# The sliding-window band cut out by two selections a job on GpSimd, in place of mask products on TensorE

## The chip, the cores and the metric

The kernel runs on one core of a Trainium2 chip (the program is built for one device). A core has five engines that run on their own instruction queues and meet only at semaphores: PE (TensorE, products), DVE (VectorE), ACT (ScalarE), POOL (GpSimd) and SP (SyncE, which here only issues DMAs). The metric is the device time of one execution in microseconds (us), as the median of several runs.

## The reference, cut to what matters

A block of attention for 8 sequences of 512 tokens with 128 features, and behind it a routed feed-forward layer over all 4096 tokens. In the attention 16 heads of 8 dimensions go two ways: a causal linear attention with a second-order feature map, and a softmax over a sliding window of 64 earlier tokens:

```python
def sliding_window_attention(q, k, v):
    B, T, H, D = q.shape
    scale = 1.0 / math.sqrt(D)
    t = jnp.arange(T)
    allowed = (t[None, :] <= t[:, None]) & (t[None, :] >= t[:, None] - WINDOW)
    scores = jnp.einsum('bqhd,bkhd->bhqk', q, k) * scale
    scores = jnp.where(allowed[None, None], scores, -jnp.inf)
    attn = jax.nn.softmax(scores, axis=-1)
    out = jnp.einsum('bhqk,bkhd->bqhd', attn, v)
    return out.reshape(B, T, H * D)
...
lin = linear_attention_causal(q_phi, k_phi, v).reshape(B, T, D_MODEL)
win = sliding_window_attention(q, k, v)
out = jnp.concatenate([lin, win], axis=-1) @ Wout
```

The feed-forward layer sends each token to two of eight experts (four with a GELU, four with a basis of squared tanh), and adds the weighted results.

## The kernel before

**Two stages.** The first half of the program (until about 530 us of the profile) is the attention, batch by batch, with the routing decisions of the batch before woven in. The second half gathers tokens by expert, tile by tile, and runs the experts. Only the first half is touched.

**The order of a batch** is written out by hand as a list of words, `ORDER`, which every engine's program follows. A capital letter is the next step of a series of this batch, a word with `-` belongs to the tail of the batch before, one with `+` to the front of the batch after:

```python
ORDER = """
M L M L M -ytr L M L M L -ycT M L M M -out L L L M -coef2 L M L +stats M +aggr P +coef L L M L L M L
M M L -h2norm P L +hT -h2T M L -logit L +q L +k mT Y L L -store P L -choose W W W +u +v -rank P
-total W +stacks +residual W -gapexp W W P W Y W W -weights +xload P W W W W Y W W P -scatter P
""".split()
```

`M` are 16 steps of scores for the running maximum ("max": four groups of four heads, four chunks of 128 keys), `L` 24 steps of the linear attention ("lin"), `W` 16 steps of the window ("win"), `P` the eight products with the values ("pv"), `Y` and `ytr` transposes of their results. pv 0 to pv 3 take the four head groups of the linear part, pv 4 to pv 7 those of the window. So from the first `W` to the last `P` a batch runs: three win jobs, u, v and rank, pv 3, the fourth win job of group 0, three of group 1, pv 4, the fourth of group 1, a transpose, two of group 2, pv 5, two of group 2, two of group 3, a transpose, two of group 3, pv 6, scatter, pv 7.

**A ring of PSUM.** Each step that PE computes for another engine is a job: it takes the next of three slots (two banks each) of `ring`. PE fills it and raises `filled`, the reader empties it and raises `freed`, and PE waits for `freed` before it fills the slot again.

**A win job** has 128 keys on the partitions, four heads, and up to 192 queries (`WQ`; 128 in the last chunk, j = 3). For each of the two banks PE first writes a mask of -1e30 outside the band with a product of the identity and `mask_win` (L1394) and then adds the scores of two heads (L1398). ACT takes the exponential into `Pb` (L846), a buffer with two halves, by n % 2; outside the band it comes out as zero. ACT's first job of a group waits for the pv that read that half last. pv (L1431) multiplies `Pb` with the values and a column of ones; for the window it waits until ACT has freed the group's last win job, and for the engine that copies `pv` out (`y_sb`: L1046 on DVE for even n, L853 on ACT for odd n).

**POOL** in the attention: for each head group of the linear part it zeroes the upper triangle of the diagonal blocks (L673, released by ACT's `freed`; raises `pd_ready`, for which pv 0 to pv 3 wait), the coefficients and the normalised rows of the next batch (`+coef`: L600 to L610, L619), the same for the feed-forward part of the batch before (`-coef2`: L600 to L610, L689), the residual of the next batch (`+residual`: L626, waits for a store of SP) and the scatter of routing records (`-scatter`: eight indirect DMAs, L698, waits for `rec_ready` of DVE). `link` makes the next POOL instruction wait for the one before through the semaphore `pool_chain`. DVE reads the max jobs with its own mask, `mask_max` (L1034), and does the routing (L1098 to L1137).

## Time and profile before

| | |
|---|---|
| time, median of 3 runs | 1073.29 us (1070.0 to 1078.98) |
| time of the profiled execution | 1078.86 us |
| its span | 1077.1 us |
| mean granted clock of PE | 0.907 of 2.4 GHz |
| busy in the span | PE 852.7, DVE 519.9, ACT 551.2, POOL 509.4 us |

The profile shows one execution. A row of a timeline gives the start and the duration in us, the engine, the line of the program, the operation, what is written and what is read (buffer numbers left out), how many instructions are merged in the row, and in brackets for how long the engine sat idle before and what ended that. PE's matmuls are pipelined: a row's duration holds the way through the array, and how fast they follow one another is seen from the starts.

### The profile page before, as it was taken

How to read it: one execution, taken by the hardware profiler on the slowest of the kernel's cores; microseconds unless marked ns; L12 is line 12 of the kernel's file. 1: busy time of each engine (PE TensorE's matmuls, PEld its weight loads, DVE VectorE, ACT ScalarE, POOL GpSimd, SP SyncE). 2: the span in 40 equal slices, each digit the busy share in tenths (PEclk: the TensorE clock that was granted, in tenths of full speed). 3: DMA queues.
4: the chain of work that ended last, by engine and by line, in shares of the span. 5: the costliest groups of instructions: out<-in, count | busy, mean ns of one | idle time of the engine just before them, and what ended most of it. 6: DMA issues, size and time to landing. Idle time of an engine off the chain costs nothing.

```text
span 1077.1 us, 23744 instructions
## 1 busy us (share of the span) xinstructions
PE 852.7 (79%) x8106; PEld 659.0 (61%) x8107; DVE 519.9 (48%) x2114; ACT 551.2 (51%) x744; POOL 509.4 (47%) x648
## 2 busy tenths in 40 slices
PE   3399997979999898989605776767999899996980
PEld 1267675756767676666503554455889877985870
DVE  5554647355564637464330111125766745766340
ACT  1476665656666665656302423326655746765240
POOL 7140635245364635242437778745545544653022
PEclk9699999989999999999856978978999988997985
DMA  2403040301213040301004545562213433332013
GB/s 44 106 2 86 5 112 2 112 5 46 71 29 89 2 116 2 111 6 32 21 11 102 87 75 82 83 179 58 70 45 98 103 92 98 101 100 52 2 13 94
DMA packets 91071, 68.50 MB, mean 64 GB/s; under 512 B 42892, under 2 KB 83274, under 8 KB 89034
## 3 DMA queue, kind: packets, MB, share of 16 engines
q1 hardware_dynamic: 74010, 55.10, 18.4%
q0 software_dynamic: 16912, 11.35, 7.5%
q8 instruction: 101, 1.65, 0.7%
q14 instruction: 48, 0.39, 0.1%
HBM read 46.86 MB, written 21.37 MB: 63 GB/s over the span
## 4 chain that ended last, share of the span: by engine, by line
PE 46%; POOL 19%; issue 13%; DVE 7%; DMA 7%; ACT 5%; another core or an unknown queue 1%; POOLq 1%; SPq 0%; DVEq 0%; ACTq 0%
PE pv L1618 8%; PE pv L1431 8%; POOL acc_d L730 7%; PE ring L1591 5%; PE ring L1394 4%; DMA acc_d<-stack,srec 4%; PE ring L1398 4%; DVE masked L1034 3%; PE ring L1442 2%; POOL stack L720 2%; ACT Pb L830 2%; PE ring L1353 2%; PE pv L1554 2%; PE ring L1322 2%; POOL c L609 2%
## 5 line engine op out<-in xcount | busy, mean ns | idle before, releaser
L730 POOL DMA_INDIRECT acc_d<-stack,srec x84 | 135.0, 1607 | 117.2 <-DVE stack L1221 79.5
L1034 DVE CUSTOM_DVE_ANT_0 masked<-ring,mask_max 128x192 bf16<-128x192 f32 (+1 forms) x512 | 141.6, 337 | 73.4 <-PE ring L1353 61.7
L1232 DVE SCALAR_TENSOR_TENSOR stack<-stack 128x512 f32<-128x512 f32 x240 | 156.9, 690 | 36.7 <-ACT stack L907 25.4
L907 ACT ACTIVATE stack<-ring,kprm 128x512 f32<-128x512 f32 x160 | 111.1, 795 | 100.0 <-DVE stack L1232 99.2
L1618 PE MATMUL pv<-stack 128*128 128x128 f32 x1120 | 136.5, 285 | 12.2 <-DVE stack L1232 7.3
L1618 PEld LDWEIGHTS pv<-stack 128*128 128x128 f32 x1120 | 133.6, 201 | 15.9 <-DVE stack L1232 8.3
L1591 PE MATMUL ring<-stack 128*128 128x256 f32 x560 | 136.9, 409 | 2.4 <-DVE stack L1232 2.4
L673 POOL TENSOR_SCALAR_AFFINE_SELECT Pb<-Pb 128x1024 f32<-128x1024 f32 x64 | 69.0, 1094 | 135.3 <-ACT Pb L830 135.2
L836 ACT ACTIVATE Pb<-ring 128x768 f32<-128x768 f32 x128 | 101.2, 812 | 61.0 <-PE ring L1382 56.6
L1591 PEld LDWEIGHTS ring<-stack 128*128 128x128 f32 x560 | 115.1, 207 | 26.7 <-DVE stack L1232 5.9
L698 POOL DMA_INDIRECT slot_d<-rec,pos x64 | 62.4, 974 | 119.6 <-DVE pos L1130 102.6
L1431 PE MATMUL pv<-Pb,vaug 128*16 128x128 f32 (+3 forms) x2816 | 118.4, 317 | 0.0
L846 ACT ACTIVATE Pb<-ring 128x768 f32<-128x768 f32 (+1 forms) x128 | 89.8, 757 | 23.4 <-PE ring L1398 20.9
L1431 PEld LDWEIGHTS pv<-Pb,vaug 128*16 128x16 f32 x2816 | 74.3, 97 | 35.7 <-issue 19.3
L1353 PE MATMUL ring<-stack 128*128 128x192 f16 (+1 forms) x512 | 63.2, 250 | 30.4 <-DMA stack<-ones 18.4
L830 ACT ACTIVATE Pb<-ring 128x1024 f32<-128x1024 f32 x64 | 63.5, 1023 | 45.0 <-PE ring L1373 37.9
L1394 PE MATMUL ring<-mask_win,identb 128*128 128x384 bf16 x256 | 81.1, 327 | 0.1
L1398 PE MATMUL ring<-stack 128*128 128x192 f16 (+1 forms) x512 | 80.5, 239 | 0.0
L1382 PE MATMUL ring<-stack 128*128 128x384 f16 (+2 forms) x384 | 64.7, 282 | 14.5 <-ACT Pb L830 7.6
L720 POOL DMA_INDIRECT stack<-n_d,grec x40 | 67.2, 1681 | 16.1 <-issue 16.1
L878 ACT ACT_TABLE_LOAD x11 | 14.1, 1283 | 106.1 <-PE pv L1554 60.9
L1353 PEld LDWEIGHTS ring<-stack 128*128 128x128 f16 x512 | 38.9, 102 | 45.4 <-issue 21.1
(205 smaller groups left out, 1261.0 us busy)
## 6 DMA issues: line engine op xcount, KB each, us to landing
stack<-L_ffn_kan_sl_W SPq DMA_DIRECT2D x20, 1024.0 KB, 5.2
stack<-hl_d SPq DMA_DIRECT2D x24, 256.0 KB
Pb<-L_ffn_mlp_W SPq DMA_DIRECT2D x22, 256.0 KB, 2.8
stack<-hl_d SPq DMA_DIRECT2D x24, 128.0 KB
hl_d<-hi SPq DMA_DIRECT2D x7, 384.0 KB, 3.1
hl_d<-lo SPq DMA_DIRECT2D x7, 384.0 KB, 3.7
xb<-L_attn_x SPq DMA_DIRECT2D x9, 256.0 KB, 5.0
acc_d<-res SPq DMA_DIRECT2D x8, 256.0 KB, 2.5
```

What stands on the lines that cost most here:

```text
L730: pool.indirect_dma_start(acc_d, bass.IndirectOffsetOnAxis(ap=srec[:, kind, u, q, 0:1], axis=0), src[:, u % 2, q, :], None, compute_op=ALU ...
L836: act.activation(Pb[:, n % 2, 2048 + 768 * hd:2048 + 768 * (hd + 1)].rearrange("p (k q) -> p k q", k=2), slot(job)[:, :, 0:384], ACT.Squar ...
L846: act.activation(Pb[:, n % 2, 768 * c:768 * (c + 1)].rearrange("p (k j q) -> p k j q", k=2, j=2)[:, :, :, 0:wq], slot(job)[:, :, 0:384].re ...
L907: act.activation(sig[z][:, g % SIGS, :], src, ACT.Sigmoid, bias=bias, scale=scale).then_inc(k_sig[z], 1)
L1034: red = dve.tensor_tensor_reduce(masked[:, (NT * n + c) % SLOTS, hh, k0:WQ], slot(job)[:, hh // 2, WQ * (hh % 2) + k0:WQ * (hh % 2 + 1)], ...
L1232: dve.scalar_tensor_tensor(basis[z][:, g % G, :], s_, -1.0, s_, ALU.add, ALU.mult).then_inc(k_bas[z], 1)
L1353: mm = pe.matmul(slot(job)[:, bk, WQ * jj + k0:WQ * (jj + 1)], sq[:, h, P * c:P * (c + 1)], sk[:, h, P * c - WIN + k0:P * (c + 1)], start= ...
L1394: pe.matmul(slot(job)[:, bk, 0:2 * WQ], identb[:], mask_win[:].rearrange("p a q -> p (a q)"), start=True, stop=True)
L1398: mm = pe.matmul(slot(job)[:, bk, WQ * jj:WQ * jj + wq], sk[:, h, P * c:P * (c + 1)], sq[:, h, P * c:P * c + wq], start=False, stop=True, ...
L1431: mm = pe.matmul(pv[32 * j:32 * j + 16, n % 2, q0:q0 + w], vaug[:, p, c, HG * (n % NHG) + j, :], src[:, j, :], start=(c == 0 and x_ == 0), ...
L1591: mm = pe.matmul(ring[:, 0, q // 2, F2 * (q % 2):F2 * (q % 2 + 1)], basis[0][:, g, P * q:P * (q + 1)], kw[u % 2][:, F2 * g:F2 * (g + 1)], ...
L1618: mm = pe.matmul(pv[:, 1, P * q:P * (q + 1)], basis[1][:, g % G, P * q:P * (q + 1)], kw[u % 2][:, 2048 + D * g:2048 + D * (g + 1)], start= ...
```

## The change

The window's mask goes from ahead of the exponential to behind it. PE no longer writes a mask into the banks; its score products start each bank region afresh. ACT's exponentials are the same. POOL, as soon as ACT has freed a win job, sets two parts of it in `Pb` to zero: queries ahead of the key (columns 0 to 127 of each head) and queries more than 64 behind it (columns 64 to 191, or 64 to 127 in the last chunk). The second selection waits for the first, since they overlap. POOL raises `pw_ready` with each job, and pv 4 to pv 7 wait for it in place of ACT's `freed`. `mask_win` and the three instructions that make it are gone.

```diff
@@ -122,7 +122,6 @@
         identf = sb("identf", [P, P])
         identb = sb("identb", [P, P], BF16)
         mask_max = sb("mask_max", [P, WQ], BF16)
-        mask_win = sb("mask_win", [P, 2, WQ], BF16)
         block = sb("block", [P, P])
         consts = sb("consts", [P, 5, NT])
         w_raw = sb("w_raw", [P, 3, D])
@@ -267,6 +266,7 @@
         mT_ready = sem("mT_ready")
         mrow_loaded = sem("mrow_loaded")
         pd_ready = sem("pd_ready")
+        pw_ready = sem("pw_ready")
         pv_done = sem("pv_done")
         y_out = [sem("y_out_dve"), sem("y_out_act")]
         ycat_ready = sem("ycat_ready")
@@ -634,13 +634,7 @@
             link(pool.memset(mask_max[:], 0.0))
             link(pool.affine_select(mask_max[:], mask_max[:], [[1, WQ]], ALU.is_ge, NEG, base=0,
                                     channel_multiplier=-1))
-            link(pool.affine_select(mask_max[:], mask_max[:], [[-1, WQ]], ALU.is_ge, NEG, base=WIN,
-                                    channel_multiplier=1))
-
-            link(pool.memset(mask_win[:], 0.0))
-            link(pool.affine_select(mask_win[:], mask_win[:], [[0, 2], [1, WQ]], ALU.is_ge, NEG, base=0,
-                                    channel_multiplier=-1))
-            pool.affine_select(mask_win[:], mask_win[:], [[0, 2], [-1, WQ]], ALU.is_ge, NEG, base=WIN,
+            pool.affine_select(mask_max[:], mask_max[:], [[-1, WQ]], ALU.is_ge, NEG, base=WIN,
                                channel_multiplier=1).then_inc(const_ready, 1)
 
             pool.memset(zero_rows, 0.0)
@@ -672,6 +666,17 @@
                         pd = Pb[:, n % 2, 1024 * j:1024 * (j + 1)].rearrange("p (a q) -> p a q", q=P)
                         pool.affine_select(pd, pd, [[0, 8], [1, P]], ALU.is_ge, 0.0, base=0,
                                            channel_multiplier=-1).then_inc(pd_ready, 1)
+                    if s == "win":
+                        job = JOBS[(s, n, j, b)]
+                        pool.wait_ge(freed[job % SLOTS], fill_no(job))
+                        pool.sem_inc(pool_at, 1)
+                        pw = Pb[:, n % 2, 768 * j:768 * (j + 1)].rearrange("p (a q) -> p a q", a=HG)
+                        last = pool.affine_select(pw[:, :, 0:P], pw[:, :, 0:P], [[0, HG], [1, P]], ALU.is_ge, 0.0,
+                                                  base=0, channel_multiplier=-1)
+                        link(last)
+                        q1 = WQ if j < NT - 1 else P
+                        pool.affine_select(pw[:, :, WIN:q1], pw[:, :, WIN:q1], [[0, HG], [-1, q1 - WIN]], ALU.is_ge,
+                                           0.0, base=0, channel_multiplier=1).then_inc(pw_ready, 1)
                     if s == "coef":
                         front_coefficients(b + 1)
                         normed()
@@ -1391,14 +1396,12 @@
                         wq = WQ if c < NT - 1 else P
                         wait_freed(pe, job)
                         for bk in range(2):
-                            pe.matmul(slot(job)[:, bk, 0:2 * WQ], identb[:],
-                                      mask_win[:].rearrange("p a q -> p (a q)"), start=True, stop=True)
                             for jj in range(2):
                                 h = HG * (n - NHG) + 2 * bk + jj
                                 mm = pe.matmul(slot(job)[:, bk, WQ * jj:WQ * jj + wq],
                                                sk[:, h, P * c:P * (c + 1)],
                                                sq[:, h, P * c:P * c + wq],
-                                               start=False, stop=True, skip_group_check=True)
+                                               start=True, stop=True)
                         mm.then_inc(filled[job % SLOTS], 1)
                     if s == "pv":
 
@@ -1409,8 +1412,7 @@
                             pe.wait_ge(freed[po_job % SLOTS], fill_no(po_job))
                         else:
 
-                            pw_job = JOBS[("win", n, NT - 1, b)]
-                            pe.wait_ge(freed[pw_job % SLOTS], fill_no(pw_job))
+                            pe.wait_ge(pw_ready, batch_no(b, NHG * NT, (n - NHG + 1) * NT))
                         pe.wait_ge(y_out[n % 2], batch_no(b, 4, LEAD + n // 2))
                         for c in range(NT):
                             parts = []
```

POOL's queue around batch 3, with what each row waits for. `res` is the residual of the next batch, `slot_d` the target of the scatter; the L673 rows are the selections of the linear part. Before, from the last lin selection of a batch to the first two of the next:

```order
L673 AFFINE_SELECT Pb<-Pb 128x1024 [waits freed0]
L626 TENSOR_SCALAR res<-xb,c 128x128 [waits x1_stored1]
L626 TENSOR_SCALAR res<-xb,c 128x128 x3
L698 DMA slot_d<-rec,pos 32768x2 [waits rec_ready]
L698 DMA slot_d<-rec,pos 32768x2 x7
L673 AFFINE_SELECT Pb<-Pb 128x1024 [waits freed2]
L673 AFFINE_SELECT Pb<-Pb 128x1024 [waits freed1]
```

After the change (the line numbers are those of the new program; L667 is the old L673, L703 the old L698), the last three win jobs of a batch and what follows them:

```order
L674 AFFINE_SELECT Pb<-Pb 128x4x128 [waits freed0]
L678 AFFINE_SELECT Pb<-Pb 128x4x128 [waits pool_chain]
L674 AFFINE_SELECT Pb<-Pb 128x4x128 [waits freed2]
L678 AFFINE_SELECT Pb<-Pb 128x4x128 [waits pool_chain]
L674 AFFINE_SELECT Pb<-Pb 128x4x128 [waits freed0]
L678 AFFINE_SELECT Pb<-Pb 128x4x64 [waits pool_chain]
L703 DMA slot_d<-rec,pos 32768x2 [waits rec_ready]
L703 DMA slot_d<-rec,pos 32768x2 x7
L667 AFFINE_SELECT Pb<-Pb 128x1024 [waits freed2]
L667 AFFINE_SELECT Pb<-Pb 128x1024 [waits freed1]
```

Between the last lin selection and the scatter there now stand 32 selections a batch, eight ahead of the residual and 24 behind it.

PE's queue at pv 4, before: the last win job ahead of it, pv 4 itself and the win job behind it.

```order
L1394 MATMUL ring<-mask_win,identb 128x384 [waits freed1]
L1398 MATMUL ring<-stack 128x192 x2
L1394 MATMUL ring<-mask_win,identb 128x384
L1398 MATMUL ring<-stack 128x192 x2
L1431 MATMUL pv<-Pb,vaug 16x192 [waits y_out_dve,freed1]
L1431 MATMUL pv<-Pb,vaug 16x192 x11
L1431 MATMUL pv<-Pb,vaug 16x128 x4
L1394 MATMUL ring<-mask_win,identb 128x384 [waits freed2]
```

After the change the same place reads (L1401 is the old L1398, L1433 the old L1431):

```order
L1401 MATMUL ring<-stack 128x192 [waits freed1]
L1401 MATMUL ring<-stack 128x192 x3
L1433 MATMUL pv<-Pb,vaug 16x192 [waits y_out_dve,pw_ready]
L1433 MATMUL pv<-Pb,vaug 16x192 x11
L1433 MATMUL pv<-Pb,vaug 16x128 x4
L1401 MATMUL ring<-stack 128x128 [waits freed2]
```

The two mask products of a job are gone, and pv waits for POOL instead of ACT.

## Rows read from the trace of the kernel before

**Rows 1.** The chain of waits in order of time: start us, us, what.

```profile
217.81 2.51 PE pv L1431 x64
...
222.16 4.04 another core or an unknown queue
...
281.87 2.51 PE pv L1431 x64
...
341.04 2.51 PE pv L1431 x64
...
520.70 2.55 PE pv L1431 x64
```

**Rows 2.** Busy time by engine in the W phase of batch 3.

```profile
core 0: us, PE busy (x) PEld busy (x) DVE busy (x) ACT busy (x) POOL busy (x), PEclk, DMA share, GB/s
262.40:284.40 22.00, 22.00 (x325) 16.40 (x324) 8.31 (x35) 14.27 (x22) 7.22 (x10) 1.00 0.45 125
```

**Rows 3.** Timeline of the same W phase: PE, ACT, DVE and SP.

```profile
263.20 0.33 PE L1394 MATMUL ring<-mask_win,identb 128*128 128x384 bf16 x1
...
263.45 2.21 ACT L846 ACTIVATE Pb<-ring 128x768 f32<-128x768 f32 x3
263.53 0.33 PE L1394 MATMUL ring<-mask_win,identb 128*128 128x384 bf16 x1
...
265.57 0.19 DVE L1106 TENSOR_TENSOR sel<-lg 128x32 bf16<-128x32 f32 x1
...
269.77 1.47 ACT L846 ACTIVATE Pb<-ring 128x512 f32<-128x512 f32 x2
...
271.62 1.39 PE L1431 MATMUL pv<-Pb,vaug 128*16 128x192 f32 x32
...
275.49 0.58 SPq L462 DMA_DIRECT2D xb<-L_attn_x  x1
...
275.79 1.39 PE L1431 MATMUL pv<-Pb,vaug 128*16 128x192 f32 x32
...
277.24 0.60 ACT L853 ACTIVATE y_sb<-pv 128x512 f32<-128x512 f32 x1 [0.49 <-PE pv L1431]
...
281.80 2.58 PE L1431 MATMUL pv<-Pb,vaug 128*16 128x192 f32 x64
```

**Rows 4.** Timeline of POOL, at the start and in batch 3.

```profile
21.51 0.52 POOL L641 TENSOR_SCALAR_AFFINE_SELECT mask_win<-mask_win 128x384 bf16<-128x384 bf16 x1
22.16 0.52 POOL L643 TENSOR_SCALAR_AFFINE_SELECT mask_win<-mask_win 128x384 bf16<-128x384 bf16 x1
...
263.02 1.79 POOL L626 TENSOR_SCALAR res<-xb,c 128x128 f32<-128x128 f32 x4 [5.34 <-DMA acc_d<-res]
...
277.45 1.05 POOL L698 DMA_INDIRECT slot_d<-rec,pos  x1 [12.64 <-DVE pos L1130]
...
287.37 2.16 POOL L673 TENSOR_SCALAR_AFFINE_SELECT Pb<-Pb 128x1024 f32<-128x1024 f32 x2
...
297.38 2.14 POOL L673 TENSOR_SCALAR_AFFINE_SELECT Pb<-Pb 128x1024 f32<-128x1024 f32 x2 [7.84 <-ACT Pb L830]
```

**Rows 5.** Selections on POOL: min/median/max ns; then groups, busy us, mean ns.

```profile
L673 POOL TENSOR_SCALAR_AFFINE_SELECT Pb<-Pb x64: 1084/1093/1112, 47.1 to 497.7; 128x1024 f32<-128x1024 f32 x64
...
L641 POOL TENSOR_SCALAR_AFFINE_SELECT mask_win<-mask_win 128x384 bf16<-128x384 bf16 x1 | 0.5, 515 | 0.1
...
L590 POOL TENSOR_SCALAR_AFFINE_SELECT block<-block 128x128 f32<-128x128 f32 x1 | 0.4, 407 | 0.1
...
L635 POOL TENSOR_SCALAR_AFFINE_SELECT mask_max<-mask_max 128x192 bf16<-128x192 bf16 x1 | 0.3, 347 | 0.1
```

**Rows 6.** Timeline of ACT and PE in the W phase of the last batch.

```profile
502.83 2.21 ACT L846 ACTIVATE Pb<-ring 128x768 f32<-128x768 f32 x3
...
510.46 1.39 PE L1431 MATMUL pv<-Pb,vaug 128*16 128x192 f32 x32
...
514.62 1.39 PE L1431 MATMUL pv<-Pb,vaug 128*16 128x192 f32 x32
```

**Rows 7.** Busy time and granted clock (PEclk) around a stall, between batches 1 and 2.

```profile
165.00:166.00 1.00, 0.00 (x0) 0.00 (x0) 0.00 (x0) 0.13 (x1) 0.00 (x0) 1.00 0.13 16
...
168.00:169.00 1.00, 1.00 (x7) 0.52 (x5) 0.44 (x3) 0.88 (x1) 0.00 (x0) 0.50 0.00 0
```

## The prediction

> **What bounds the kernel now.** I read four views of the profile, in this order. First the chain of waits [rows 1]: in each of the eight batches it passes through the block of 64 matmuls that is pv 6 and pv 7 together, and these blocks lie 59.17 us apart in the undisturbed step from batch 3 to batch 4 (281.87 to 341.04). So the first half of the program is one chain on PE's in-order queue, and what makes pv 7 of a batch late makes everything behind it late. Second, the window of batch 3 in which its 16 win jobs run, "the W phase" below [rows 2]: in 22.00 us PE is marked busy all the time, ACT 14.27, POOL 7.22. PE looks like the bound. Third, the timeline of that window [rows 3] says how far: a mask product and the two score matmuls of a bank take 0.33 us together (263.20 to 263.53), so a win job with its two banks costs PE 0.65 us; ACT's three exponentials in a row take 2.21 us, 0.74 us a job. PE and ACT are nearly equal, and the mask is half of PE's part. Fourth, POOL's own timeline [rows 4]: between its residual step (from 263.02) and its scatter (from 277.45) POOL does nothing, and pv 4 to pv 7 don't wait for it.
>
> **What is removed.** 256 mask products on PE, 32 a batch. I estimate its part of the 0.33 us at half, 0.163 us, since it has as many columns (384) as the two score products together: 5.2 us a batch and 42 us in all. That is not the gain. ACT still needs up to 0.74 us a job, 11.8 us a batch, for the same exponentials. Without masks pv 5 could come about 1.0 us earlier (three jobs with six masks lie between pv 4 and pv 5), and pv 7 about 2.1 us earlier, when ACT's last exponential would end near 281.0: at most 17 us over eight batches, if nothing took PE's place. Removing the building of the mask saves three short POOL instructions at the start (two of them start at 21.51 and 22.16 [rows 4]), some 1.8 us, while nobody needs POOL before the first lin selection at 47.1 [rows 5]. I cost it at nothing; were it on the path, it would be a gain of 1.8 us.
>
> **What is added, per job.** Two selections on POOL, the second waiting for the first through POOL's chain semaphore. The trace has no selection of 4 x 128 f32, so I bound it [rows 5]: 384 elements in two rows take 515 ns, 1024 in eight rows 1093 ns (all 64 between 1084 and 1112). Between them a line has 0.90 ns an element: 512 elements take 631 ns, call it 635. A 4 x 64 one, by the same line down to 256 elements, 400 ns. Lower end: 515, for 384 elements, since 512 can't be cheaper. Upper end: the `block` selection took 407 ns for 128 elements in a pattern of 16 short rows, which is some 120 ns above that line; added to 631 it is 750 ns. I take 635, as both neighbours have whole rows of 128 or 192 like the new ones.
>
> The Trainium skill (GPSIMD Engine Reference, section 3.1) gives two paces that differ: 1.8 cycles an element at 1.2 GHz for a tight loop, which is 768 ns for 512 elements, and about one cycle for a compare and select. By the first the sum below would be near +70 us instead of +50; the 1093 ns for 1024 elements in rows 5 speaks for the second.
>
> The wait between linked selections is 0.135 us: the two on `mask_win` start 0.65 us apart (21.51, 22.16) and one takes 0.515. Selections that aren't linked overlap by about 0.045 us: a pair takes 2.14 to 2.16, not 2.19 [rows 4]. So a job of 4 x 128 and 4 x 128 takes 0.635 + 0.135 + 0.635 - 0.045 = 1.37 us (1.36 to 1.37), the fourth of a group (4 x 64 in the second) 1.15, and a group of four 5.26 us. Sixteen jobs: 21.0 us. POOL's residual of 4 x 0.45 = 1.8 us lies behind the fourth job. POOL has 22.8 us to do in a W phase in which, from the first exponential's end to pv 7, there are 18.9 us. **POOL becomes the bound there.**
>
> **The schedule of batch 3 after the change**, in times of the old trace. An exponential is ready for POOL about 0.15 us after its end. Group 0: three exponentials start at 263.45, so POOL starts at 264.4 and is through three jobs at 268.5. The fourth comes only behind pv 3, which the routing chain on DVE (until 265.57) and `u`, `v` hold where they are; its exponential starts at 269.77 now, 0.13 earlier then, and ends near 270.25, so POOL has it at 270.4 and ends at 271.55. pv 4 starts at 271.65, where it starts now (271.62 [rows 3]): nothing lost, nothing won. The residual ends at 273.35. Group 1's exponentials are all ready long before POOL: 273.35 + 5.26 = 278.6, and pv 5 starts at 278.75 instead of 275.79, 2.95 us late. Group 2: two jobs until 281.35; the third needs its exponential, which ACT can run only behind pv 5 and its copy of pv (pv 5 takes 1.3 us, the copy starts 1.45 us behind pv 5's start [rows 3] and takes 0.6: pv 5 ends at 280.05, copy to 280.8, exponential to 281.55), so POOL goes on at 281.7 and ends the group at 284.2. pv 6 follows at once. Group 3: 284.2 + 5.26 = 289.45, and pv 7 starts at 289.6. Now it starts in the middle of the block at 281.80, at 283.1. **So 6.5 us are lost per batch.**
>
> In the last batch there is no residual step. Its three exponentials start at 502.83 and pv 4 stands at 510.46, pv 5 at 514.62 [rows 6]. The same steps give: POOL has the fourth job from 509.2 to 510.35, pv 5 at 515.75, the third job of group 2 from 518.7, group 2 ends at 521.2, group 3 at 526.45, pv 7 at 526.6 instead of 521.9: 4.7 us.
>
> Sum: 7 x 6.5 + 4.7 = 50.2 us.
>
> **What else moves.** POOL's scatter stands behind the 16 jobs. It takes 10 us (277.45 to 287.37) and then starts near 289.5 instead of 277.45, and the two lin selections of the next batch end near 301.7 instead of 289.5. The next thing that somebody needs from POOL is the pair of lin selections at 297.38 [rows 4] (behind it stand coef2, n2 and the coefficients of the next front, which are on the chain). That pair is released by ACT, which is 6.5 us late itself: 303.9. So 2.2 us of cover are left of 7.8; if they are gone, each further us on POOL costs one us a batch. In the last batch scatter ends near 536.6, just before coef2 of that batch is due, so a fraction of a us can be lost there too. SP's load of xb waits for the residual, but stands behind the stacks' loads and starts at 275.49, later than 273.35: no cost. The stacks' loads wait for pv 3 only.
>
> **The clock.** PE now waits 3.9 us before pv 7 and about 3 us before pv 5. The old trace shows what such a stall does: between batch 1 and batch 2 PE had no work in 165 to 166, and in 168 to 169 the granted clock was 0.50, 1.2 GHz, instead of 2.4 [rows 7]. What it costs I read from the steps between the pv blocks: batch 2 to 3 took 64.06 us, of which 4.04 are the stall at 222.16, against 59.17 undisturbed: 0.85 us. Some steps between batches have such a fall already. I take 0.5 us for each batch, 4 us. Lower end nothing; upper end pv 5 and pv 7 both at half speed (1.3 us more each) and 0.9 in what follows, 3.5 us a batch.
>
> The total is +54 us. The profiled execution has a span of 1077.1 and a time of 1078.86, 5.6 above the median of the runs, 1073.29. Against its own time: 1133; against the median, 1127.5. I predict 1128.
>
> **Rivals.** (a) *POOL keeps pace* and the time falls. pv 7 must not be later than 283.1: from 270.4 on 13 jobs and the residual fit in 12.6 us only if a job takes 0.83 us, 0.37 us a selection. The nearest row is 515 ns for 384 elements, already too long. If selections were free the time would be 1073 - 17 = 1056. For it speaks only that 42 us leave PE. 5%. (b) *The clock* falls for pv 5 and pv 7 in every batch: 1073.3 + 50.2 + 28 = 1151. 10%. (c) *DVE is held up by the selections.* The last DVE step of the routing ahead of pv 3 is at 265.57 [rows 3], beside the first jobs; were three of them held for a selection each, pv 3 and all behind it would be 1.9 us later: 15 us more, 1143. Against it: the 64 selections of 1084 to 1112 ns ran beside DVE work and differ by 3%. 5%. The Trainium skill (SBUF — State Buffer, "SBUF: two separate sides") has such a rule: VectorE and GpSimd share a port pair as an exclusive lock when VectorE reads two SBUF inputs or runs in a two-port mode. By it, (c) would happen. (d) *The wait is hidden*, within 1%, because POOL's delay is made good by something that waits now and PE, freed of masks, catches up in the L and M steps. Nothing shows it: there PE has no masks to lose. It would give 1073. 4%. The forecast holds 76%.
>
> **How the numbers follow.** Low end: selections of 515 ns give a job of 1.12, a group of 4.35, pv 7 4.1 us late in seven batches and 2.3 in the last, 31 us, no clock: 1104. High end: 750 ns give a group of 6.1, pv 7 8.9 and 7.1 us late, 70 us, and 16 us of clock (2 us a batch): 1159, which covers (b) and (c). Left out are (a), (d) and a tail. A change of under 1%, 11 us, is about what a measurement of this kernel can't tell from none. Faster 0.05, within 1% 0.04, slower 0.91.
>
> **What would show it.** In the new trace: the new selections with mean near 635 ns (4 x 64: 400); POOL without a gap in the W phase from 273 on; PE idle before L1433 (pv) with POOL as releaser, about 3 us and 4 us a batch, some 50 us in all; pv 6 and pv 7 no longer one block but 4 us apart; steps between pv 7s of 65 to 66 us. It is wrong if selections take under 400 ns, if POOL idles in the W phase, or if the loss stands in the L and M part (then scatter was late, or the clock).

## The result and the profile after

The changed kernel takes 1135.02 us (median of 5 runs, 1132.23 to 1150.37) where the kernel before, on the same chip, takes 1075.01 (5 runs, 1070.0 to 1078.98). The ratio is 1.0571, interval 1.0509 to 1.0632: 60 us slower. Forecast were 1128 and slower. The ratios, here and below, leave out runs that fell into a slower state (here the one at 1150.37); medians and ranges are of all runs.

The page of the changed kernel: span; busy time, share and instructions of each engine; PE's granted clock in tenths over 40 slices; the chain that ended last by engine; two rows of the groups (busy, mean ns of one, idle time ahead and what ended it).

```profile
span 1140.9 us, 23611 instructions
PE 846.9 (74%) x7850; PEld 646.2 (57%) x7851; DVE 538.5 (47%) x2114; ACT 549.1 (48%) x744; POOL 657.1 (58%) x901
PEclk9798998989899898998975688888899998998885
PE 39%; POOL 26%; issue 14%; DVE 9%; ACT 5%; DMA 4%; POOLq 1%; SPq 0%; DVEq 0%; ACTq 0%
L1433 PE MATMUL pv<-Pb,vaug 128*16 128x128 f32 (+3 forms) x2816 | 137.8, 348 | 64.2 <-POOL Pb L678 63.1
L674 POOL TENSOR_SCALAR_AFFINE_SELECT Pb<-Pb 128x512 f32<-128x512 f32 x128 | 81.5, 637 | 87.3 <-ACT Pb L851 87.3
```

pv now waits 63.1 us for POOL's second selection. It is where the forecast put the loss, and near its size (some 50 us).

The two lines of selections, with all durations (min/median/max in ns), and two of the waits that belong to them (sum in us, count, longest):

```profile
L674 POOL TENSOR_SCALAR_AFFINE_SELECT Pb<-Pb x128: 628/634/688, 79.0 to 581.0; 128x512 f32<-128x512 f32 x128
L678 POOL TENSOR_SCALAR_AFFINE_SELECT Pb<-Pb x128: 414/634/672, 79.7 to 581.7; 128x512 f32<-128x512 f32 x96, 128x256 f32<-128x256 f32 x32
...
PE pv L1433 <- POOL Pb L678: 63.1, 31, 3.6
ACT y_sb L858 <- PE pv L1433: 126.0, 32, 7.0
```

A 4 x 128 selection takes 634 ns (forecast 635, read off the line through the two neighbours of [rows 5]), a 4 x 64 one 414 (forecast 400).

The timeline of one W phase, batch 4: start, duration, engine, line, what it writes and reads, how often, and in brackets the idle time ahead of it and what ended it. It answers to [rows 3].

```profile
352.62 0.19 DVE L1104 TENSOR_TENSOR lg<-lg,sc 128x32 f32<-128x32 f32 x1
...
352.91 2.21 ACT L851 ACTIVATE Pb<-ring 128x768 f32<-128x768 f32 x3
...
353.88 0.63 POOL L674 TENSOR_SCALAR_AFFINE_SELECT Pb<-Pb 128x512 f32<-128x512 f32 x1 [6.75 <-ACT Pb L851]
353.96 0.59 DVE L1104 TENSOR_TENSOR lg<-lg,sc 128x32 f32<-128x32 f32 x1
354.58 0.63 POOL L678 TENSOR_SCALAR_AFFINE_SELECT Pb<-Pb 128x512 f32<-128x512 f32 x1
354.59 0.67 DVE L1105 TENSOR_TENSOR lg<-lg,prefer 128x32 f32<-128x32 f32 x1
355.17 0.63 POOL L674 TENSOR_SCALAR_AFFINE_SELECT Pb<-Pb 128x512 f32<-128x512 f32 x1
355.29 0.19 DVE L1106 TENSOR_REDUCE sc<-lg 128x4 f32<-128x32 f32 x1
355.51 0.33 DVE L1107 TENSOR_TENSOR lg<-prefer,sc 128x32 f32<-128x32 f32 x1
...
355.88 0.67 DVE L1111 TENSOR_TENSOR sel<-lg 128x32 bf16<-128x32 f32 x1
...
361.87 1.39 PE L1433 MATMUL pv<-Pb,vaug 128*16 128x192 f32 x32 [0.78 <-POOL Pb L678]
...
368.62 2.55 PE L1433 MATMUL pv<-Pb,vaug 128*16 128x192 f32 x32 [3.50 <-POOL Pb L678]
371.22 0.60 ACT L858 ACTIVATE y_sb<-pv 128x512 f32<-128x512 f32 x1 [4.88 <-PE pv L1433]
...
375.39 1.39 PE L1433 MATMUL pv<-Pb,vaug 128*16 128x192 f32 x32 [0.28 <-POOL Pb L678]
...
380.33 2.55 PE L1433 MATMUL pv<-Pb,vaug 128*16 128x192 f32 x32 [3.55 <-POOL Pb L678]
...
396.69 2.13 POOL L667 TENSOR_SCALAR_AFFINE_SELECT Pb<-Pb 128x1024 f32<-128x1024 f32 x2 [4.01 <-ACT Pb L835]
```

Four things are to be seen. pv 4, 5, 6 and 7 (361.87, 368.62, 375.39, 380.33) each wait for POOL, and pv 6 and pv 7, one block of 64 before, stand 4.94 us apart. POOL runs a job in 353.88 to 355.17, 1.29 us: 0.70 from the first selection to the linked one and 0.59 to the next job. Four of DVE's routing steps with two inputs are stretched beside the selections: three take 0.59 to 0.67 us (353.96, 354.59, 355.88), and one that starts in the middle of a selection takes 0.33 (355.51). Each ends 0.04 to 0.05 us after the selection that runs beside it. The same L1104 took 0.19 just ahead of them (352.62), the `sel` step took 0.19 in [rows 3], and the step with one input beside a selection (355.29) takes 0.19 too. And pv 5 and pv 7 take 2.55 us where pv 4 and pv 6 take 1.39.

The windows around pv 5 and pv 7 (stretch, length; busy time of PE, PEld, DVE, ACT, POOL; then granted clock, DMA share, GB/s) tell what slowed them:

```profile
368.00:370.00 2.00, 1.38 (x20) 0.84 (x24) 0.00 (x0) 0.00 (x0) 1.86 (x5) 0.67 0.72 200
370.00:372.00 2.00, 2.00 (x27) 1.28 (x20) 0.00 (x0) 0.64 (x2) 1.08 (x2) 0.50 0.28 70
...
378.00:380.00 2.00, 0.00 (x0) 0.00 (x0) 0.00 (x0) 0.00 (x0) 1.86 (x4) 0.73 0.00 0
380.00:382.00 2.00, 1.67 (x24) 0.93 (x28) 0.00 (x0) 0.00 (x0) 1.35 (x3) 0.50 0.00 0
```

PE has no work ahead of 368.6 and of 380.3, and the granted clock falls to 0.50, 1.2 GHz, for the block behind each wait. In this execution 15 blocks of pv 5 or pv 7 stand behind a wait of 3.4 to 3.6 us, and 13 of them are stretched in full. No block is stretched behind the waits of 0.3 to 1.8 us at pv 4, pv 6 and the last pv 5.

### Where the 60 us stand

The steps from one pv block's start to the next, read from PE's timelines. "Per batch" is an undisturbed batch, "all 8" the sum over the program, after minus before.

| step | before | after | per batch | all 8 | forecast, all 8 |
|---|---|---|---|---|---|
| pv 7 to the next pv 0 | 17.03 | 19.01 | +1.98 | -1.1 | clock, in 4 |
| pv 0 to pv 2 | 18.71 | 18.7 | 0 | +2.3 | 0 |
| pv 2 to pv 3 | 6.70 | 7.65 | +0.95 | +6.2 | 0 |
| pv 3 to pv 4 | 5.01 | 4.85 | -0.16 | +0.5 | 0 |
| pv 4 to pv 5 | 4.16 | 6.75 | +2.59 | +19.0 | +21.6 |
| pv 5 to pv 6 | 6.01 | 6.70 | +0.69 | +4.1 | in the next row |
| pv 6 to pv 7 | 1.19 | 4.93 | +3.74 | +29.8 | +28.4 for both |
| sum (with -0.4 before batch 0) | | | +9.8 | +60.3 | +54 |

At the last pv 7 the changed kernel is 60.3 us behind (582.1 against 521.8); the half behind it, which the change doesn't touch, adds 3.5 of the 63.8 between the two spans. One row doesn't fit the others: the step from pv 7 to the next pv 0 has grown by 1.98 us where nothing disturbs it, yet over all it is 1.1 shorter. In the kernel before, four of these seven steps hold a stall of 2.7 to 5.2 us, 14.9 in all (one is the stall of [rows 1]); in this execution of the changed kernel they hold next to none. What those stalls are comes back below, and is not settled.

The last batch, which has no residual step on POOL, differs: from pv 2 to pv 7 it takes 7.2 us more than before, where the forecast had 4.7. pv 3 comes 1.5 us late, and its 56 matmuls then take 3.85 us (560.17) where they took 2.36 before, which puts pv 4 1.6 us later still.

### The profile page after: what moved, and what is told of

Same layout as the page of the kernel before. It is cut to its first block, busy times and chain, and to the rows that moved or that the text cites. A ratio compares the mean times of both kernels' runs of the same rounds, so it can differ in the third digit from the quotient of the medians.

```text
span 1140.9 us, 23611 instructions
## 1 busy us (share of the span) xinstructions
PE 846.9 (74%) x7850; PEld 646.2 (57%) x7851; DVE 538.5 (47%) x2114; ACT 549.1 (48%) x744; POOL 657.1 (58%) x901
## 3 DMA queue, kind: packets, MB, share of 16 engines
q1 hardware_dynamic: 74010, 55.10, 17.1%
## 4 chain that ended last, share of the span: by engine, by line
PE 39%; POOL 26%; issue 14%; DVE 9%; ACT 5%; DMA 4%; POOLq 1%; SPq 0%; DVEq 0%; ACTq 0%
PE pv L1620 10%; PE pv L1433 8%; PE ring L1593 7%; POOL acc_d L735 6%; POOL Pb L674 5%; POOL Pb L678 4%; DMA acc_d<-stack,srec 3%; DVE masked L1039 3%; POOL stack L725 2%; PE ring L1358 2%; ACT Pb L835 2%; PE ring L1378 2%; PE ring L1444 1%; POOL c L609 1%; PE ring L1387 1%
## 5 line engine op out<-in xcount | busy, mean ns | idle before, releaser
L1433 PE MATMUL pv<-Pb,vaug 128*16 128x128 f32 (+3 forms) x2816 | 137.8, 348 | 64.2 <-POOL Pb L678 63.1
L1433 PEld LDWEIGHTS pv<-Pb,vaug 128*16 128x16 f32 x2816 | 79.1, 103 | 113.2 <-POOL Pb L678 70.2
L1593 PE MATMUL ring<-stack 128*128 128x256 f32 x560 | 134.1, 403 | 2.8 <-DVE stack L1237 2.4
L674 POOL TENSOR_SCALAR_AFFINE_SELECT Pb<-Pb 128x512 f32<-128x512 f32 x128 | 81.5, 637 | 87.3 <-ACT Pb L851 87.3
L667 POOL TENSOR_SCALAR_AFFINE_SELECT Pb<-Pb 128x1024 f32<-128x1024 f32 x64 | 68.8, 1093 | 78.5 <-ACT Pb L835 78.5
L1358 PE MATMUL ring<-stack 128*128 128x192 f16 (+1 forms) x512 | 64.4, 254 | 29.2 <-DMA stack<-ones 18.2
L858 ACT ACTIVATE y_sb<-pv 128x512 f32<-128x512 f32 x32 | 19.1, 598 | 126.0 <-PE pv L1433 126.0
L678 POOL TENSOR_SCALAR_AFFINE_SELECT Pb<-Pb 128x512 f32<-128x512 f32 (+1 forms) x128 | 74.4, 581 | 8.8
L703 POOL DMA_INDIRECT slot_d<-rec,pos x64 | 62.2, 972 | 26.7 <-issue 18.7
L725 POOL DMA_INDIRECT stack<-n_d,grec x40 | 66.9, 1671 | 16.1 <-issue 16.1
L1358 PEld LDWEIGHTS ring<-stack 128*128 128x128 f16 x512 | 39.9, 103 | 44.7 <-issue 21.6
```

Of the source, the lines that this page charges most:

```text
L674: last = pool.affine_select(pw[:, :, 0:P], pw[:, :, 0:P], [[0, HG], [1, P]], ALU.is_ge, 0.0, base=0, channel_multiplier=-1)
L678: pool.affine_select(pw[:, :, WIN:q1], pw[:, :, WIN:q1], [[0, HG], [-1, q1 - WIN]], ALU.is_ge, 0.0, base=0, channel_multiplier=1).then_inc ...
L725: pool.indirect_dma_start(dst[:, u % n, q, :], None, source, bass.IndirectOffsetOnAxis(ap=grec[:, kind, u % RECS, q, 0:1], axis=0)).then_i ...
L1358: mm = pe.matmul(slot(job)[:, bk, WQ * jj + k0:WQ * (jj + 1)], sq[:, h, P * c:P * (c + 1)], sk[:, h, P * c - WIN + k0:P * (c + 1)], start= ...
L1433: mm = pe.matmul(pv[32 * j:32 * j + 16, n % 2, q0:q0 + w], vaug[:, p, c, HG * (n % NHG) + j, :], src[:, j, :], start=(c == 0 and x_ == 0), ...
L1593: mm = pe.matmul(ring[:, 0, q // 2, F2 * (q % 2):F2 * (q % 2 + 1)], basis[0][:, g, P * q:P * (q + 1)], kw[u % 2][:, F2 * g:F2 * (g + 1)], ...
```

## The experiments

The theory: POOL's 32 selections a batch set the pace of the W phase. What it left to test: (1) what the masks' removal is worth by itself; (2) whether the clock at 1.2 GHz behind the waits costs something; (3) whether the selections hold DVE up; (4) whether the loss goes when a job is cheap enough for POOL. Each run is given with the kernel before on its own chip.

### Neither masks nor selections

From the changed kernel the POOL branch goes, and pv waits for ACT again:

```diff
-                    if s == "win":
-                        ...
...
-                            pe.wait_ge(pw_ready, batch_no(b, NHG * NT, (n - NHG + 1) * NT))
+                            pw_job = JOBS[("win", n, NT - 1, b)]
+                            pe.wait_ge(freed[pw_job % SLOTS], fill_no(pw_job))
```

> Neither mask products nor selections: scores outside the band reach the values, so the window's result is another one, and the routing behind it may differ; read the first half of the program, up to the last pv 7. Theory (POOL's selections pace the W phase of each batch): without them PE and ACT pace it, pv 7 comes about 2 us a batch before that of the kernel before; last pv 7 near 505 us (522.0 before, 582.1 after), time near 1056 if the second half has as many tiles. Rival (most of the loss is not POOL's pace but PE's half clock by itself): the first half stays long, over 540.

1032.56 us, ratio 0.9535 (0.9479 to 0.9591) to the kernel before at 1086.84. This run and the next three are from one chip, which is not that of the first profiles. PE's timeline of pv 4, pv 5 and the joined pv 6 and 7 in one batch:

```profile
260.13 1.39 PE L1423 MATMUL pv<-Pb,vaug 128*16 128x192 f32 x32
...
263.32 1.39 PE L1423 MATMUL pv<-Pb,vaug 128*16 128x192 f32 x32
...
268.35 2.58 PE L1423 MATMUL pv<-Pb,vaug 128*16 128x192 f32 x64
```

The steps into pv 3, pv 4, pv 5 and pv 6 are shorter than before by 0.13, 1.0, 1.0 and 1.0 us: the masks' removal alone is worth 3.1 us a batch, 25 us in all, where 2 us a batch were expected. The last pv 7 stands at 494.2 (expected 505), 27.6 us ahead of the first profile of the kernel before. The whole time can't be compared: routed by other values, the second half has fewer tiles (80 scatters into `acc_d` instead of 84, 36 gathers from `n_d` instead of 40). The waits at pv 5 and pv 7 are gone with the selections, and with them the 2.55-us blocks: both hang on POOL. The rival, PE's half clock by itself, is out.

### PE kept busy ahead of pv 5 and pv 7

Products that nobody reads, into the bank that pv overwrites:

```diff
                     if s == "pv":
+                        if n in (5, 7):
+                            pe.wait_ge(y_out[n % 2], batch_no(b, 4, LEAD + n // 2))
+                            for _ in range(14):
+                                pe.matmul(pv[:, n % 2, :], sk[:, 0, 0:P], sk[:, 0, 0:T], start=True, stop=True)
```

> The changed kernel with 14 products of 512 columns (3.0 us at full clock) on PE ahead of the wait of pv 5 and of pv 7; they write the pv bank, which pv then starts afresh. Theory (the loss has two parts, the wait for POOL and the half clock that PE is granted behind it): the waits stay, but pv 5 and pv 7 take 1.3 us instead of 2.55, the step from pv 7 to the next pv 0 falls from 19.0 to 17.0, and the time falls by some 15 to 25 us, to 1112 to 1122. Rival (the clock costs nothing, the wait is all): 1135 or a little more.

1149.71 us, ratio 1.0526 (1.0444 to 1.0608). The same steps as in the timeline above, now with the filler ahead (from one batch's pv 5 to the next batch's pv 0):

```profile
364.14 3.19 PE L1410 MATMUL pv<-stack 128*128 128x512 f16 x14
367.80 1.39 PE L1437 MATMUL pv<-Pb,vaug 128*16 128x192 f32 x32 [0.47 <-POOL Pb L678]
...
378.11 1.39 PE L1437 MATMUL pv<-Pb,vaug 128*16 128x192 f32 x32 [0.42 <-POOL Pb L678]
...
395.14 2.36 PE L1437 MATMUL pv<-Pb,vaug 128*16 128x128 f32 x56
```

pv 5 and pv 7 take 1.39 us again, the step from pv 7 to pv 0 is 17.03 (378.11 to 395.14) instead of 19.01, and that from pv 5 to pv 6 is 5.37 instead of 6.70. So the clock did cost up to 3.3 us a batch by these two steps; an undisturbed batch takes 65.9 us from pv 7 to pv 7, where the changed kernel has 68.3 to 69.6. But the time doesn't show it: the ratio is within the noise of the changed kernel's 1.0571. Five of the batches are 2.6 to 4.6 us longer than the undisturbed one, some 19 us in all, and the last pv 7 stands at 583.0, where the changed kernel, on another chip, has it at 582.1. The expected gain of 15 to 25 us is a miss; the mechanism is seen in the steps.

### POOL held until the routing is through

```diff
                     if s == "win":
+                        if n == NHG and j == 0 and b > 0:
+                            pool.wait_ge(sel_ready, b)
```

> The changed kernel, where POOL's first selection of batches 1 to 7 waits until DVE has written sel, the last step of the routing ahead of pv 3. Theory (DVE's instructions with two inputs in SBUF are held while a selection runs, and that makes pv 3 0.95 us late): sel takes 0.19 us again, the step from the first exponential to pv 3 falls from 4.1 to 3.2 us, POOL still has time for three jobs ahead of the fourth, time 6 to 8 us less: near 1128. Rival (pv 3's delay has another cause, or POOL's later start costs as much as it saves): 1135 or more.

1142.38 us, ratio 1.0510 (1.0442 to 1.0578). ACT, DVE, POOL and PE ahead of pv 3 of one batch:

```profile
145.58 2.21 ACT L853 ACTIVATE Pb<-ring 128x768 f32<-128x768 f32 x3
...
147.53 0.19 DVE L1113 TENSOR_TENSOR sel<-lg 128x32 bf16<-128x32 f32 x1
147.92 0.63 POOL L676 TENSOR_SCALAR_AFFINE_SELECT Pb<-Pb 128x512 f32<-128x512 f32 x1 [8.11 <-DVE sel L1113]
148.62 1.71 PE L1435 MATMUL pv<-Pb,vaug 128*16 128x128 f32 x32
```

With no selection beside it the `sel` step takes 0.19 us, and pv 3 follows 3.04 us behind the exponentials' start. In the changed kernel pv 3 starts at 357.02, 4.11 us behind them (352.91). The step from pv 2 to pv 3 is 6.57 in each of batches 1 to 6, where the changed kernel has 7.65 in most (6.14 instead of 7.66 in the last). So the selections do hold DVE up, for about 1 us a batch. The time was expected to fall by 6 to 8 us. The ratio is 0.6% below the changed kernel's, but their intervals overlap, and the last pv 7 stands at 584.5, 2.4 us later than in the first profile of the changed kernel: the gain is not resolved.

All eight `sel` steps, min/median/max in ns, in the kernel before and in the changed one:

```profile
L1106 DVE TENSOR_TENSOR sel<-lg x8: 191/191/193, 139.1 to 541.9; 128x32 bf16<-128x32 f32 x8
```

```profile
L1111 DVE TENSOR_TENSOR sel<-lg x8: 193/669/670, 148.3 to 603.9; 128x32 bf16<-128x32 f32 x8
```

191 ns against 669. The Trainium skill (SBUF — State Buffer, "SBUF: two separate sides") has a port pair that VectorE and GpSimd share as an exclusive lock when VectorE reads two SBUF inputs. By that rule the trace agrees: the stretched steps are those with two inputs, and each ends just behind the selection beside it, the one of 0.33 us too.

### Masks and selections both

The mask products are back on PE as before (so is the making of `mask_win`, not shown), and the selections stay.

```diff
+                        masked_pe = True
                         for bk in range(2):
+                            if masked_pe:
+                                pe.matmul(slot(job)[:, bk, 0:2 * WQ], identb[:],
+                                          mask_win[:].rearrange("p a q -> p (a q)"), start=True, stop=True)
                             ...
-                                               start=True, stop=True)
+                                               start=not masked_pe, stop=True, skip_group_check=masked_pe)
```

> The changed kernel with the mask products back on PE, and the selections kept: both do the band. Theory (POOL paces the W phase, so the 42 us that leave PE are worth nothing there): not slower than the changed kernel, 1130 to 1140; if PE's extra work keeps its clock up, a little less, 1120 to 1130. Rival (the masks' removal gave back a part of what POOL costs): slower, 1150 or more.

1146.87 us, ratio 1.0551 (1.0489 to 1.0612): the changed kernel again. pv 5 and pv 7 of the last but one batch, with their waits:

```profile
514.23 1.94 PE L1444 MATMUL pv<-Pb,vaug 128*16 128x192 f32 x32 [2.52 <-POOL Pb L685]
...
525.97 1.39 PE L1444 MATMUL pv<-Pb,vaug 128*16 128x192 f32 x32 [2.72 <-POOL Pb L685]
```

PE does 256 products more and waits 1.0 and 0.8 us less here than the 3.49 and 3.55 us of the changed kernel; over the program its waits for POOL fall from 63.1 to 41.1 us. While POOL sets the pace, taking the mask products (by the forecast's estimate 42 us) from PE buys nothing measurable. The last pv 7 stands at 588.8, 6.6 us later than in the changed kernel on another chip, with stalls of 1.4 to 5.7 us at four of the batch starts, so this rests on the ratio and on the waits.

### One selection a job

The second selection goes, so the window is wider than the reference's, and the tokens are routed by other values.

```diff
-                        last = pool.affine_select(pw[:, :, 0:P], pw[:, :, 0:P], [[0, HG], [1, P]], ALU.is_ge, 0.0,
-                                                  base=0, channel_multiplier=-1)
-                        link(last)
-                        q1 = WQ if j < NT - 1 else P
-                        pool.affine_select(pw[:, :, WIN:q1], pw[:, :, WIN:q1], [[0, HG], [-1, q1 - WIN]], ALU.is_ge,
-                                           0.0, base=0, channel_multiplier=1).then_inc(pw_ready, 1)
+                        pool.affine_select(pw[:, :, 0:P], pw[:, :, 0:P], [[0, HG], [1, P]], ALU.is_ge, 0.0,
+                                           base=0, channel_multiplier=-1).then_inc(pw_ready, 1)
```

> The changed kernel with one selection a job: the queries ahead of the key are zeroed, those more than 64 behind are not, so the window is wider than the reference's; the routing and with it the second half may differ. Read the steps between the pv blocks of the first half. Theory (POOL paces only while a job takes it more than about 0.83 us): a job takes 0.6 us, POOL keeps up, pv 4 to 5 is near 3.3 us and pv 6 to 7 near 1.2 to 1.8, as without selections; only pv 2 to 3 keeps a part of the lock's delay; last pv 7 at 500 us or a little before. Rival (any wait of pv for POOL costs, through the semaphore's way or POOL's order): pv 6 to 7 over 2.5 and last pv 7 over 540.

1120.99 us, ratio 0.9823 (0.9792 to 0.9855). This run and the next three are from a chip on which the kernel before takes 1142.13 us (11 runs, 1138.1 to 1147.41), called the slower chip below. The time of this kernel says nothing of the sign: its second half too has 80 scatters and 36 gathers instead of 84 and 40. The steps do.

```profile
280.73 3.65 POOL L674 TENSOR_SCALAR_AFFINE_SELECT Pb<-Pb 128x512 f32<-128x512 f32 x6
...
283.18 1.39 PE L1429 MATMUL pv<-Pb,vaug 128*16 128x192 f32 x32 [0.82 <-POOL Pb L674]
...
290.18 1.39 PE L1429 MATMUL pv<-Pb,vaug 128*16 128x192 f32 x32 [0.58 <-POOL Pb L674]
```

Unlinked selections run at 0.61 us each (3.65 for six), so a job costs 0.61, below the 0.83 that the prediction gave as the point from which POOL keeps pace. The waits for POOL shrink to 0.3 to 0.8 us, no block is stretched, and the steps from pv 3 to pv 7 take 4.37, 4.07, 5.03 and 1.97: 15.4 us, against 16.4 before and 23.2 in the changed kernel. DVE is still held: pv 2 to pv 3 takes 7.29, where it was 6.70 before, so that from pv 2 to pv 7 only 0.3 us a batch are won. With the work on POOL halved the loss is gone, as the theory has it, but hardly a gain is left. The last pv 7 stands at 556.7, where 500 was expected: this and the three other kernels profiled on this chip need 25.3 to 29.2 us from pv 7 to the next pv 0 in six of the seven steps, where it was 17 to 19 elsewhere. No trace of the kernel before is from this chip, so how much of that it has there too is not known.

### Filler and held start together

Both edits above in one kernel.

> The changed kernel with both cures at once: products ahead of the waits of pv 5 and pv 7, and POOL's first selection behind sel. Theory (the loss of 9.9 us a batch in undisturbed steps is 6 us of POOL's pace, 0.95 us of held DVE instructions and 3 us of clock): steps 2 to 3 6.6, 7 to 0 17.0, 5 to 6 5.4, so a batch takes some 3.8 us less than in the changed kernel; time 1105 to 1125, the width being stalls at the start of a batch. Rival (the parts overlap, what one cure wins the other loses): steps no shorter than with one cure.

1200.71 us, ratio 1.0510 (1.0476 to 1.0544). In its one undisturbed batch the effects add: 64.8 us from pv 7 to pv 7 (103.1 to 167.9), the steps 6.57, 5.37 and 17.04 as in the two single runs. Later batches have 26 to 29 us behind pv 7. In time, where 1105 to 1125 us were expected, nothing is won: 5.1% over the kernel before on its chip, a miss.

### The work divided between PE and POOL

POOL has time for some jobs: it is free from the residual on [rows 4]. In these kernels a few win jobs, listed in place of `ON`, are selected on POOL and the others masked on PE:

```diff
+                        masked_pe = (n, j) not in ON
                         for bk in range(2):
+                            if masked_pe:
+                                pe.matmul(slot(job)[:, bk, 0:2 * WQ], identb[:],
+                                          mask_win[:].rearrange("p a q -> p (a q)"), start=True, stop=True)
```

and in POOL's branch

```diff
-                    if s == "win":
+                    if s == "win" and (n, j) in ON:
```

pv waits for ACT or for POOL, as its group needs.

First six jobs, group 1 j = 0, 1 and the whole of group 2:

> Six of the sixteen win jobs of a batch are cut by POOL (group 1, j = 0 and 1; group 2, all four), the other ten by mask products on PE. Theory (the masks' removal is worth 0.33 us a job between two pv blocks as long as POOL has finished before pv comes there): step 3 to 4 0.65 us shorter than before the change, 4 to 5 0.65, 5 to 6 0.15 to 0.65, no clock loss; 12 to 15 us faster than the kernel before, ratio 0.985 to 0.99. Rival (PE's masks were hidden behind ACT): ratio 1.00.

1161.84 us, ratio 1.0163 (1.0126 to 1.0200). Then six jobs spread further, group 1 j = 0, 1, group 2 j = 0 to 2, group 3 j = 0:

> As the mixed version, with POOL's six jobs chosen by when pv comes: group 1, j = 0 and 1; group 2, j = 0 to 2; group 3, j = 0. Theory: step 3 to 4 0.65 us shorter than before the change, 4 to 5 0.65, 5 to 6 0.65, 6 to 7 unchanged; 16 us faster than the kernel before, ratio near 0.985. Rival: POOL's job of group 3 is late and makes pv 7 wait; step 6 to 7 over 1.5 us, ratio 0.99 to 1.00.

1160.33 us, ratio 1.0152 (1.0118 to 1.0185). Within the W phase both do what was expected: pv 3 to pv 7 take 4.56, 3.51, 5.6 to 5.8 and 1.19 us, 15.1 or less, with no wait for POOL. In time both miss: ratios of 0.985 to 0.99 were expected. From pv 7 to the next pv 0 they take 27.6 to 28.3 us in six of seven steps. The six-job kernel there:

```profile
221.94 2.35 PE L1449 MATMUL pv<-Pb,vaug 128*16 128x192 f32 x53
222.46 1.05 POOL L710 DMA_INDIRECT slot_d<-rec,pos  x1 [0.17 <-issue]
...
224.45 0.51 PE L1449 MATMUL pv<-Pb,vaug 128*16 128x192 f32 x6 [0.16 <-issue]
...
225.19 0.42 PE L1449 MATMUL pv<-Pb,vaug 128*16 128x128 f32 x5 [0.23 <-issue]
...
231.41 0.96 POOL L710 DMA_INDIRECT slot_d<-rec,pos  x1 [0.30 <-issue]
...
233.85 0.60 ACT L865 ACTIVATE y_sb<-pv 128x512 f32<-128x512 f32 x1 [11.05 <-remote]
235.06 1.04 PE L1385 MATMUL ring<-stack 128*128 128x128 f16 x8 [5.18 <-DVE maxima L1046]
```

PE's own block is broken up: 53 of the 64 matmuls of pv 6 and pv 7 end at 224.29, the other 11 at 225.61, with idle time between them in which PE waited for nothing that the profile shows ("issue"). ACT's copy of pv 7 starts only at 233.85, and the profile has no releaser in this core for it ("remote"); POOL's scatter goes on meanwhile. I took it that a scatter that starts beside pv 7 is what stalls, since in these kernels it starts there. A set on a further chip was to tell (it did not fall on the slower one), with the kernel before and the changed one again for comparison:

> The kernel before, unchanged, on the chip of this set, for its trace. Time ratio 1.00. Where the chip is one on which it takes over 1100 us, its trace shows what is longer there: by the one theory the step from pv 7 to the next pv 0 (17.0 us undisturbed), in which ACT and PE stand while POOL issues the scatter; all other steps as in the profile of before. Rival: a slower second half, or a lower clock everywhere.

1072.47 us, ratio 1.0045 (1.0006 to 1.0085) to the other runs of the same kernel (1072.7): half a per cent is what this comparison cannot tell.

> The changed kernel, unchanged, on the same chip. Steps 2 to 3, 4 to 5, 5 to 6 and 6 to 7 as in its first profile (7.65, 6.75, 6.7, 4.93), 3.0 us of selections and clock; ratio 1.05 to 1.06. If stalls at a batch's start hang on the chip, they are alike in both kernels, and the difference of the last pv 7 minus the stalls is 9.9 us times the undisturbed batches.

1141.24 us, ratio 1.0664 (1.0577 to 1.0750), a little over the 1.05 to 1.06 expected; its last pv 7 is 62.7 us behind the kernel before on that chip (580.1 against 517.4), with the steps of the table above from pv 2 on; from pv 7 to pv 0 it takes 18.05 to 19.01 in six steps and 20.97 in one. There too the seven steps from pv 7 to pv 0 add up to nearly the same in both kernels (2 us apart), since the kernel before has four with stalls of 1.6 to 4.0 us. The loss repeats.

> The version with six jobs on POOL (group 1, j = 0 and 1; group 2, j = 0 to 2; group 3, j = 0) again, beside the trace of the kernel before. Its steps between pv 3 and pv 7 are 1.5 us shorter than before the change. Theory (the scatter, which stands behind the selections on POOL, starts some 5 us later and so stands at the batch's start, where PE and ACT then stall): its step from pv 7 to pv 0 is longer than that of the kernel before on the same chip; ratio 1.00 to 1.02. Rival (the stall is the chip's and not the scatter's): ratio 0.985 to 0.99 and equal steps from pv 7 to pv 0.

1070.97 us, ratio 0.9975 (0.9936 to 1.0014): the kernel that lost 1.5% on the slower chip loses nothing here, and wins nothing: the ratio lies between the two that were expected. Its step from pv 7 to pv 0 is 17.1, with only two stalls in the program, although the scatter starts beside pv 7 as it did there. So the scatter's place alone does not make the stall, and on this chip that theory falls; whether it adds to it on the slower one stays open. The last pv 7 stands at 501.2, 16.1 us ahead of the kernel before: 12 us are the 1.5 us a batch of the moved work, the rest mostly fewer stalls. Yet the time is the same, because the second half, counted from POOL's first gather of tokens, takes 528.9 us instead of 510.3. Its groups, and those of the kernel before on the same chip behind them:

```profile
L1636 PE MATMUL pv<-stack 128*128 128x128 f32 x1120 | 140.9, 291 | 21.7 <-issue 16.7 <-DVE stack L1244 4.9
L1609 PE MATMUL ring<-stack 128*128 128x256 f32 x560 | 135.6, 407 | 7.7 <-issue 5.7 <-DVE stack L1244 2.0
```

```profile
L1618 PE MATMUL pv<-stack 128*128 128x128 f32 x1120 | 134.5, 283 | 11.5 <-DVE stack L1232 6.5 <-issue 4.9
L1591 PE MATMUL ring<-stack 128*128 128x256 f32 x560 | 135.6, 407 | 2.2 <-DVE stack L1232 2.2
```

The same matmuls, with 22.4 us of idle time ended by "issue" instead of 4.9. Last, four jobs on POOL, groups 1 and 2, j = 0, 1:

> Four jobs on POOL (group 1 and group 2, j = 0 and 1), which are done about when the scatter of the kernel before begins, so that the scatter stays where it was. Theory (later scatter makes the stall longer): steps 3 to 4 0.45 and 4 to 5 0.65 us shorter than before the change, step from pv 7 to pv 0 as in the kernel before on this chip; ratio 0.985 to 0.995, below the version with six jobs. Rival: as slow as the version with six jobs.

1072.77 us, ratio 1.0010 (0.9980 to 1.0039), where 0.985 to 0.995 was expected; the last pv 7 at 504.3, 13 us ahead, 9 of them in the steps where work was moved; the second half 518.6 instead of 510.3. No division tried beats the kernel before in time, though on this chip both reach the last pv 7 earlier.

## Why the prediction was right, and where its sizes were off

**POOL becomes the bound: right.** POOL's selections are the releaser of 63.1 us of PE's waiting, the waits before pv 5 and pv 7 are 3.50 and 3.55 us (forecast about 3 and 3.9), pv 6 and pv 7 came apart, and pv 3 to pv 4 is 4.85 instead of 5.01. The runs without selections and with one a job are the other side of it. One reading was off: pv 4 was to start where it did, 8.17 us behind the first exponential, and starts 8.96 behind it (352.91 to 361.87), since pv 3 is late and with it POOL's fourth job.

**The selections: 635 forecast, 634 measured (4 x 64: 400 and 414 ns); their distance not.** The link was taken at 0.135 us, from two selections at the start that don't run in this place. Here a linked one starts 0.70 us behind one of 0.63, a gap of 0.07. A job is 1.29 us instead of 1.37, a group 4.93 (the step from pv 6 to pv 7) instead of 5.26, and pv 4 to pv 5 gave 19.0 instead of 21.6 us. pv 5 to pv 7 gave 33.9 instead of 28.4: POOL's part of it shrank too, but some 9 us of clock stand in these steps, which the forecast booked elsewhere; with the filler they give 3.2 us a batch, 26 in all. pv 5 at half speed delays ACT's copy, and with it the third job of group 2 (371.22 in the timeline).

**The clock: under-sized in the term, and the total came near by luck.** It was costed at 0.5 us a batch, since one stall of 4.04 us before had cost 0.85. In fact both waits took the clock to 1.2 GHz in nearly every batch, which is rival (b), with up to 3.3 us a batch as the filler run shows, near the upper end of 3.5. Against the filler's steps the seven steps from pv 7 to pv 0 hold some 14 us of it and those from pv 5 to pv 6 some 9: about 23 us, where the sum had 4. Against that stand the 14.9 us of stalls at batch starts that the kernel before has and this one hardly does. The forecast had no term for that: it carried the stalls along as the kernel's own. The two errors, +19 and -15 us, nearly cancel, and 1128 against 1135 is as near as that by luck.

**DVE beside the selections: wrong.** Rival (c) had 5%, and is real: 0.95 us a batch, 6.2 us over the program (forecast as its price 1.9 and 15). The failed step is the evidence against it: that 64 selections take 1084 to 1112 ns says that POOL isn't held; whether DVE is, only the durations of DVE's own steps beside them can say. Three steps up to `sel` are stretched by 0.40 to 0.48 us each, not by a whole selection as that rival put it, and a fourth by 0.14. It does not decide the sign.

**What the masks cost PE: low.** At most 17 us were given; without masks and selections 3.1 us a batch go, 25 us. The forecast let only pv 5 and pv 7 profit; in the trace pv 4, pv 5 and pv 6 each come 1.0 us nearer. But the run with both shows that none of it counts while POOL is late, so this error cost nothing here.

**The scatter: right.** POOL waits 4.01 us for ACT ahead of the next pair of lin selections (396.69), 7.84 before [rows 4], where the forecast left 2.2. Its cover holds, and more is left than forecast since POOL is through its groups sooner.

**Left open.** What stalls PE, ACT and DVE for 3 to 5 us at some batch starts, and for 9 to 11 on the slower chip, is not shown: the profile gives "remote" or "issue", and the place of the scatter, the one suspect that was tried, does not explain it alone. A suspect that was not tried is the loading of instructions: in the six-job kernel's stall the record of such a load of 16 KB, at 224.8, lasts 2.1 us where most last 0.9 to 1.5, but one at 283.9 in the kernel before lasts 2.4 and nothing stalls there. Nor is it shown why the second half gets 8 to 19 us longer in the two divided kernels, whose program for that half is the same. Both sizes are those of the gains looked for, so differences of under some 15 us in this kernel can be argued from steps and not from the time alone. Why the divided kernels lose 1.5% on the slower chip cannot be read without a trace of the kernel before from there. Whether another form of DVE's routing steps would escape the hold was not tried.

## What to carry to other kernels

Before moving work to an idle engine, lay its new work against the stretch in which it has to be done: POOL was idle for 53% of the program before, and had 18.9 us for 21.5 us of work (22.8 by the forecast) in the phase that counted. Keeping pace decides: at 0.61 us a job pv 3 to pv 7 is 1.0 us shorter than before, at 1.29 it is 6.9 us longer, and as long as POOL is late, what PE saves is worth nothing. Then price what the new work sets off: nearly every wait of 3.4 to 3.6 us here also halved PE's clock for the block behind it, and the selections made some DVE steps beside them three times as long. Look for both in the durations of the neighbours, not in those of the moved work.

## What the runs showed of the hardware

- A selection in place on POOL takes 634 ns for 128 x 4 x 128 f32 and 414 for 128 x 4 x 64; one that waits for the one ahead on its own queue starts 0.07 us behind its end.
- While POOL selects, DVE operations of 128 x 32 with two inputs in SBUF take up to 0.67 us instead of 0.19 and end 0.04 to 0.05 us after the selection beside them; ahead of the selections they take 0.19, and one with a single input takes 0.19 beside them too.
- Behind 13 of 15 waits of 3.4 to 3.6 us PE's granted clock was 0.50 for the next block, and its 32 matmuls took 2.55 us instead of 1.39; with products that nobody reads ahead of the wait, which left 0.4 to 0.5 us idle, they took 1.39.
- The kernel before took 1072.5 to 1086.8 us in three sets of runs and 1142.1 on the slower chip. The four edited kernels profiled there spent 25.3 to 29.2 us instead of 17 in one step of most batches, with waits that the profile puts down to nothing of this core.
